# Cross-attention, two layers: row maxima sent in three parts, stack loads reordered on SyncE, bulk loads in ScalarE's queue

## The chip, the cores and the metric

One NeuronCore of a Trainium2 chip runs the whole kernel as one launch. The metric is the device time of that launch in microseconds (us). The engines are TensorE (PE in the profile; PEld is its weight load), VectorE (DVE), ScalarE (ACT), GpSimd (POOL) and SyncE (SP, which only issues DMAs). Two of them issue DMAs here, SyncE and ScalarE, each in a queue of its own over the same 16 DMA engines.

## The reference

```python
# 2 layers, batch 16, L = S = 128, D = 256, 32 query heads over 8 key/value heads, head size 8
for W in (layer0, layer1):
    q = x @ W.q + W.bq                    # (16, 128, 256)
    k = ctx @ W.k + W.bk                  # (16, 128, 64)
    v = ctx @ W.v + W.bv
    scores = einsum(q, k) / sqrt(8) + mask
    attn = softmax(scores, axis=-1)
    out = (attn @ v) @ W.o + W.bo + x
    x = layernorm(out) * gamma + beta     # the input of the next layer's q
```

The mask is all zeros for these inputs; the kernel looks at it and takes the branch without it. The context is the same in both layers.

## The kernel before, in words

A unit is one batch element of one layer: u = 0 to 31, layer 0 first. Every engine runs its own program over phases t, and the phases of the engines are tied together by semaphores alone. The order in each program is written out by hand. In phase t:

- TensorE runs the eight `scores(t, kv)`, one for each key/value head, into three banks `s_bank` (L567), four matmuls each. Between them it runs eight `scoresT` (L587), the transposed scores of the unit before, for ScalarE's exponential. At fixed places between these it runs `probs_v` of units t-3 and t-2 (L647), `transpose_max(t-1)` (L634), `project(t+3)` (L613 to L623), `project_out(t-3)` (L663) and, from phase 4 to 19, `transpose_y`.
- VectorE takes the maximum of each `s_bank` (L460). After the third of a phase it runs `max_rows(t-1)` (L468 to L471). That splits the transposed maxima of unit t-1 into three bf16 parts, high, mid and low; high has been written by ScalarE (`max_first`, L390). Each part is 32 heads by 128 columns.
- GpSimd splits q and k of unit t+3 into three bf16 parts each (L190 to L193) and does the rest of the layer norm.
- SyncE, in its iteration t, issues in this order: the rows of maxima of unit t-1 (L256), once `max_rows(t-1)` has ended; from phase 20 the result of unit t-4 (L260); the two stacks of unit t+2 (L243 and L248); the parts of unit t+3 (L228, and in layer 0 three for k, L232); and at some iterations a bulk load.

The scores are computed from stacks. q and k are each a sum of three bf16 parts, and the nine products of parts lie on 72 rows of the contraction (`TERM_ROWS`). The parts go to DRAM (`q_scratch`, `k_scratch`) and come back spread over 72 partitions: `q_stack` 576 KB, `k_stack` 144 KB for each unit, in a ring of 4 slots. `scores(u, 0)` waits for `stacks_loaded` of its slot. Rows 72 to 74 of `q_stack` hold the three parts of the maxima, with ones in `k_stack`, so that `scoresT` comes out with the maximum taken off. The first `scoresT` of unit u waits for `max_rows_loaded`; it is the last `scoresT` of phase u+1.

A DMA's wait stands on SyncE ahead of its issue, so everything behind it on SyncE waits too:

```python
need(sp, scoresT_ready, KV * (u - RING + 1))     # load_stacks(u): the slot is free
sp.wait_ge(q_stored[two], 16 * (u // 2 + 1))     # load_stacks(u): the parts are in DRAM
sp.wait_ge(maxT_step, MAXT_STEPS * (u + 1))      # load_max_rows(u): L255
sp.wait_ge(ln_step, LN_STEPS * (u + 1))          # store_y(u)
```

Of the kernel before, what the change touches and what calls it, by code (L numbers as in the profile page):

```python
# [13 lines left out]
P = 128  # L14
LAYERS, BATCH, L, S, D = 2, 16, 128, 128, 256
HEADS, KV, HD = 32, 8, 8
# [12 lines left out]
LAG = 15  # L29
AHEAD = 3  # L30
V_AHEAD = 1
X_GROUP = 4
S_BANKS = 3
INPUT_GROUPS = ((0, 1), (1, 2), (2, 4), (4, 8), (8, 12), (12, 16))
MAXT_STEPS, FLIP_STEPS, NORM_STEPS, LN_STEPS = 3, 3, 4, 4
STACK_DMAS = 2
LEAD = KT * D
VW = 4 * HD

# [9 lines left out]
def reads_before(u):  # L49

    return 6 * min(u, BATCH) + 4 * max(u - BATCH, 0)


def input_group(b):
    return next(n for n, (first, end) in enumerate(INPUT_GROUPS) if first <= b < end)


def need(engine, sem, count):
# [5 lines left out]
def cross_attention(nc, x, inputs, mask, lead, w_q1, w_kv, w_o, rows, out):  # L64
    with ExitStack() as ctx:
# [74 lines left out]
        wq1_loaded = sem("wq1_loaded")  # L140
        wkv_loaded = sem("wkv_loaded")
        bv_loaded = sem("bv_loaded")
        rows_loaded = sem("rows_loaded")
        wo_loaded = sem("wo_loaded")
        masks_loaded = sem("masks_loaded")
        x_loaded = sems("x_loaded", BATCH // X_GROUP)
        inputs_loaded = sems("inputs_loaded", len(INPUT_GROUPS))
        stacks_loaded = sems("stacks_loaded", RING)
        q_stored = sems("q_stored", 2)
        k_stored = sems("k_stored", 2)  # L150
# [59 lines left out]
        block = ctx.enter_context(nc.Block())  # L210
        rows_d = rows.rearrange("(a n) -> a n", a=LAYERS)

        def load_inputs(engine, group):
            first, end = INPUT_GROUPS[group]
            engine.dma_start(in_sb[:, first:end].rearrange("p b a k l -> p (b a k l)"),
                             inputs[:, first:end].rearrange("p b a k l -> p (b a k l)")).then_inc(inputs_loaded[group], 16)

        @block.sync
        def _(sp):
            sp.dma_start(lead_sb[:], lead).then_inc(lead_loaded, 16)  # L220
            sp.dma_start(wkv_sb[:].rearrange("p k a n -> p (k a n)"), w_kv).then_inc(wkv_loaded, 16)
            sp.dma_start(mask_sb[:].rearrange("p b s -> p (b s)"), mask).then_inc(masks_loaded, 16)
            load_inputs(sp, 2)

            def store_parts(u):
                two = u % 2
                sp.wait_ge(q_split[two], PARTS * (u // 2 + 1))
                sp.dma_start(q_scratch[u].rearrange("a p n -> p a n"), q_parts[:, two]).then_inc(q_stored[two], 16)  # L228
                if u < BATCH:
                    sp.wait_ge(k_split[two], PARTS * (u // 2 + 1))  # L230
                    for part in range(PARTS):
                        sp.dma_start(k_scratch[u, :, :, part].rearrange("a d (h s) -> (a d) h s", h=KV),  # L232
                                     k_parts[:, two, part]).then_inc(k_stored[two], 16)

            def load_stacks(u):
                layer, b = place(u)
                slot, two = u % RING, u % 2

                need(sp, scoresT_ready, KV * (u - RING + 1))
                if u < RING:  # L240
                    sp.wait_ge(k_padded, 1)
                sp.wait_ge(q_stored[two], 16 * (u // 2 + 1))
                sp.dma_start(q_stack[0:TERM_ROWS, slot].rearrange("p h l -> p (h l)"),  # L243
                             q_scratch[u].rearrange("a (d h) n -> (a d) (h n)", d=HD).unsqueeze(1)
                             .broadcast_to([PARTS * HD, PARTS, HEADS * L])).then_inc(stacks_loaded[slot], 16)
                if layer == 0:
                    sp.wait_ge(k_stored[two], 16 * PARTS * (u // 2 + 1))
                sp.dma_start(k_stack[0:TERM_ROWS, slot].rearrange("p h l -> p (h l)"),  # L248
                             k_scratch[b, layer].rearrange("d a n -> (d a) n").partition_broadcast(PARTS)
                             ).then_inc(stacks_loaded[slot], 16)  # L250

            def load_max_rows(u):
                slot, two = u % RING, u % 2
                need(sp, scoresT_ready, KV * (u - RING + 1))
                sp.wait_ge(maxT_step, MAXT_STEPS * (u + 1))  # L255
                sp.dma_start(q_stack[TERM_ROWS:STACK_ROWS, slot], max_parts[:, two]).then_inc(max_rows_loaded[two], 16)  # L256

            def store_y(u):
                sp.wait_ge(ln_step, LN_STEPS * (u + 1))
                sp.dma_start(out[u - BATCH], y[:, u % 2]).then_inc(y_left[u % 2], 16)  # L260

            for t in range(-AHEAD, UNITS + 5):
                if live(t - 1):
                    load_max_rows(t - 1)
                if BATCH <= t - 4 < UNITS:
                    store_y(t - 4)
                if live(t + 2):
                    load_stacks(t + 2)
                if live(t + AHEAD):
                    store_parts(t + AHEAD)  # L270
                if t in (-2, 2, 6):
                    load_inputs(sp, 3 + (t + 2) // 4)
                if t == 0:
                    sp.dma_start(rows_sb[:], rows_d[:, 0:3 * D].partition_broadcast(P)).then_inc(rows_loaded, 16)
                if t > 0 and t % X_GROUP == 1 and t < BATCH:
                    sp.dma_start(x_sb[:, t - 1:t - 1 + X_GROUP],
                                 x[t - 1:t - 1 + X_GROUP].rearrange("b l d -> l b d")).then_inc(x_loaded[t // X_GROUP], 16)
                if t == 1:
                    sp.dma_start(wo_sb[:].rearrange("p a k n -> p (a k n)"), w_o).then_inc(wo_loaded, 16)
                if t == 3:  # L280
                    sp.dma_start(wq1_sb[:], w_q1).then_inc(wq1_loaded, 16)

            for two in range(2):
                sp.wait_ge(y_left[two], 16 * BATCH // 2)
                sp.wait_ge(q_stored[two], 16 * UNITS // 2)
                sp.wait_ge(k_stored[two], 16 * PARTS * BATCH // 2)

        @block.gpsimd
        def _(pool):
# [39 lines left out]

            def add_bo(u):  # L330
                layer, b = place(u)
                if u == 0:
                    pool.wait_ge(rows_loaded, 16)
                if layer == 0 and b % X_GROUP == 0:
                    pool.wait_ge(x_loaded[b // X_GROUP], 16)
                if layer == 1:
                    pool.wait_ge(ln_step, LN_STEPS * (b + 1))
                need(pool, norm_step, NORM_STEPS * (u - 1) + 1)
                nc.gpsimd.tensor_tensor(x_bo[:], x_sb[:, b], rows_sb[:, layer, 0:D], ALU.add).then_inc(x_bo_ready, 1)  # L339
# [14 lines left out]
        def _(act):  # L354
# [31 lines left out]
            def max_first(u):  # L386

                act.wait_ge(maxT_ready, u + 1)
                need(act, max_rows_loaded[u % 2], 16 * (u // 2))
                nc.scalar.activation(max_parts[0:HEADS, u % 2], maxT_ps, ACT.Copy).then_inc(max_high, 1)  # L390

            def norm(u):
# [10 lines left out]
            def sum_mask():  # L403

                act.wait_ge(masks_loaded, 16)
                act.wait_ge(sum_cleared, 1)
                nc.scalar.activation(probs[:, 0, 0:KV // 2].rearrange("p h n -> p (h n)"),
                                     mask_sb[:].rearrange("p b s -> p (b s)"), ACT.Abs,
                                     accum_out=mask_sum[:, 0:1]).then_inc(sum_found, 1)

            act.wait_ge(lead_loaded, 16)
            nc.scalar.activation(bq_scaled[:], lead_sb[:, LEAD:LEAD + LAYERS * KT], ACT.Copy,
# [2 lines left out]
            for t in range(-AHEAD, UNITS + 5):  # L415
# [21 lines left out]
                exp(g + 7)  # L437
                if 0 <= t - 4 < BATCH:
                    copy_yT(t - 4)

        @block.vector
        def _(dve):
# [113 lines left out]
        def _(pe):  # L556
# [19 lines left out]
            def scoresT(g, masked):  # L576
# [5 lines left out]
                    pe.wait_ge(qk_read, reads_before(AHEAD))  # L582
                    pe.wait_ge(v_ready, 2)
                if kv == 0:
                    pe.wait_ge(max_rows_loaded[two], 16 * (u // 2 + 1))
                need(pe, exp_done, g - 1)
                mm = nc.tensor.matmul(t_bank[kv % 2][:], k_stack[0:STACK_ROWS, slot, kv],  # L587
                                      q_stack[0:STACK_ROWS, slot, GROUP * kv:GROUP * (kv + 1)],
# [7 lines left out]
            def project(u):  # L596
# [8 lines left out]
                    pe.wait_ge(qk_read, reads_before(u))  # L605
                    need(pe, v_ready, 2 * min(u - 2, BATCH))
                need(pe, yT_copied, min(u - AHEAD - 4, BATCH))
                if layer == 0 and b == INPUT_GROUPS[input_group(b)][0]:
                    pe.wait_ge(inputs_loaded[input_group(b)], 16)
                w = (lead_sb if layer == 0 else wq1_sb)[:, 0:LEAD].rearrange("p (k n) -> p k n", k=KT)  # L610
                for n in range(KT):
                    for k in range(KT):
# [40 lines left out]
            def project_out(u, t):  # L653
                layer = u // BATCH
                pe.wait_ge(flip_step, FLIP_STEPS * (u + 1))
                if u == 0:
                    pe.wait_ge(wo_loaded, 16)
                if live(t - 1):
                    pe.wait_ge(maxT_step, MAXT_STEPS * t)
                else:  # L660
                    need(pe, norm_step, NORM_STEPS * (u - 1) + 1)
                for k in range(KT):
                    mm = nc.tensor.matmul(proj_ps, attnT[:, k], wo_sb[:, layer, k], start=(k == 0), stop=(k == KT - 1))  # L663
                mm.then_inc(proj_ready, 1)
# [96 lines left out]
```

## Time and profile before

| | us |
|---|---|
| median of 3 runs | 340.6 (338.73 to 343.22) |
| the profiled execution | 340.19 |
| its span, first to last instruction | 338.3 |
| mean granted TensorE clock | 0.93 of full |

The profile is of one execution. Its span leaves out 1.9 us around the first and last instruction (340.19 - 338.3). A busy time is the sum of an engine's instructions, and what an engine waited for is put down to the event that came last. The clock is given as a share of full: 1.00 is 2.4 GHz and 0.50 is 1.2 GHz, and a value between them in a stretch is a mix of the two.

### The profile page before, as it was taken

What the parts mean: (1) busy time and instruction counts of PE and PEld (TensorE: products, weight loads), DVE (VectorE), ACT (ScalarE), POOL (GpSimd) and SP (SyncE); (2) the same over time, 40 slices, a digit from 0 to 9 for tenths busy, and PEclk for the clock granted to TensorE, in tenths of its full rate; (3) what the DMA queues carried; (4) which work ended last, traced back from release to release, by engine and by line L of the source; (5) the groups of instructions that cost most, each with busy time, mean ns of one, the idle gap of its engine ahead of it and who ended that gap; (6) DMA issues with size and microseconds to landing.
All of it is one profiled execution on the core that took longest, in us unless ns stands there. A gap on an engine that the chain in (4) does not pass through costs nothing.

```text
span 338.3 us, 8301 instructions
## 1 busy us (share of the span) xinstructions
PE 292.6 (86%) x2890; PEld 196.8 (58%) x2890; DVE 271.5 (80%) x625; ACT 209.1 (62%) x500; POOL 194.0 (57%) x335
## 2 busy tenths in 40 slices
PE   7466399599998999999899999999999999888851
PEld 4366276277666776776566666666666666554320
DVE  4426449489988998999899999999999999999441
ACT  3601257277766777777677777777777777656540
POOL 6123305366766776776656666666666666444464
PEclk9756769699999999999999999999999999999795
DMA  7584766714674446344634434444444444420000
GB/s 280 168 237 114 213 182 179 212 31 122 182 242 135 118 124 183 100 125 131 178 101 112 115 109 120 126 121 137 132 119 121 137 141 130 122 64 18 20 16 31
DMA packets 34555, 44.40 MB, mean 131 GB/s; under 512 B 11857, under 2 KB 28241, under 8 KB 31697
## 3 DMA queue, kind: packets, MB, share of 16 engines
q1 hardware_dynamic: 33952, 43.27, 44.7%
q8 instruction: 25, 0.41, 0.5%
q10 hardware_dynamic: 560, 0.59, 0.5%
q14 instruction: 18, 0.14, 0.1%
HBM read 33.10 MB, written 9.96 MB: 127 GB/s over the span
## 4 chain that ended last, share of the span: by engine, by line
PE 37%; DVE 35%; DMA 14%; issue 9%; SPq 2%; ACT 1%; POOL 1%; POOLq 0%; ACTq 0%; DVEq 0%
DVE row_max L460 18%; DMA q_stack<-max_parts 9%; PE misc_bank L663 8%; PE s_bank L567 7%; PE t_bank L587 7%; PE oT_bank L647 7%; DVE o_sb L481 4%; DMA q_scratch<-q_parts 4%; PE qkv_bank L613 3%; DVE z L499 3%; DVE attnT L492 3%; DVE max_parts L468 2%; DVE recip L487 2%; PE qkv_bank L619 2%; PE qkv_bank L623 1%
## 5 line engine op out<-in xcount | busy, mean ns | idle before, releaser
L460 DVE TENSOR_REDUCE row_max<-s_bank 128x4 f32<-128x512 f32 x256 | 168.8, 678 | 35.9 <-PE s_bank L567 35.0
L365 ACT ACTIVATE probs<-t_bank 128x512 f32<-128x512 f32 x256 | 148.0, 601 | 77.8 <-PE t_bank L587 77.4
L587 PE MATMUL t_bank<-q_stack,k_stack 75*128 75x512 bf16 x256 | 99.8, 393 | 20.4 <-DMA q_stack<-max_parts 12.6
L567 PE MATMUL s_bank<-k_stack,q_stack 72*128 72x128 bf16 x1024 | 102.3, 225 | 8.2 <-DMA k_stack<-k_scratch 7.4
L567 PEld LDWEIGHTS s_bank<-k_stack,q_stack 72*128 72x128 bf16 x1024 | 76.2, 101 | 53.1 <-issue 18.5
L307 POOL TENSOR_TENSOR rstd<-var_eps,minus_half 128x1 f32<-128x1 f32 x32 | 17.6, 548 | 56.0 <-DVE var_eps L507 56.0
L316 POOL TENSOR_TENSOR attn<-o_sb,recip 128x256 f32<-128x256 f32 x32 | 20.0, 625 | 40.0 <-DVE recip L487 39.7
L587 PEld LDWEIGHTS t_bank<-q_stack,k_stack 75*128 75x128 bf16 x256 | 25.0, 99 | 28.4 <-ACT probs L365 13.1
L663 PE MATMUL misc_bank<-wo_sb,attnT 128*128 128x256 f32 x128 | 36.0, 405 | 5.7 <-DVE attnT L492 5.7
L190 POOL TENSOR_TENSOR q_rest<-qT,q_parts 128x256 f32<-128x256 f32 x30 | 20.1, 669 | 34.4 <-ACT q_parts L374 34.4
L374 ACT ACTIVATE qT<-qkv_bank,bq_scaled 128x128 f32<-128x128 f32 x60 | 22.1, 369 | 22.6 <-PE qkv_bank L623 20.8
L647 PE MATMUL oT_bank<-probs,v_later 128*32 128x256 f32 x512 | 35.1, 393 | 0.1
L647 PE MATMUL oT_bank<-probs,v_ones 128*32 128x256 f32 x512 | 35.1, 393 | 0.0
L663 PEld LDWEIGHTS misc_bank<-wo_sb,attnT 128*128 128x128 f32 x128 | 23.5, 196 | 14.6 <-DVE attnT L492 11.9
L395 ACT ACTIVATE normed<-z,shift,rstd 128x256 f32<-128x256 f32 x32 | 19.1, 597 | 14.9 <-POOL shift L309 14.9
L323 POOL TENSOR_TENSOR scaled<-normed,rows_sb 128x256 f32<-128x256 f32 x32 | 23.3, 728 | 0.7 <-ACT normed L395 0.7
L339 POOL TENSOR_TENSOR x_bo<-x_sb,rows_sb 128x256 f32<-128x256 f32 x32 | 23.4, 732 | 0.0
L481 DVE STREAM_TRANSPOSE o_sb<-oT_bank 128x512 f32<-128x512 f32 x32 | 22.6, 707 | 0.2 <-PE oT_bank L647 0.2
L374 ACT ACTIVATE q_parts<-qkv_bank,bq_scaled 128x128 bf16<-128x128 f32 x60 | 22.4, 373 | 0.0
L647 PEld LDWEIGHTS oT_bank<-probs,v_ones 128*32 128x32 f32 x512 | 13.5, 110 | 14.5 <-issue 8.6
L647 PEld LDWEIGHTS oT_bank<-probs,v_later 128*32 128x32 f32 x512 | 13.5, 110 | 14.4 <-issue 8.2
L193 POOL TENSOR_TENSOR q_parts<-q_rest,q_parts 128x256 bf16<-128x256 f32 x30 | 20.1, 669 | 2.4
(76 smaller groups left out, 359.2 us busy)
## 6 DMA issues: line engine op xcount, KB each, us to landing
q_stack<-q_scratch SPq DMA_DIRECT2D x32, 576.0 KB
q_scratch<-q_parts SPq DMA_DIRECT2D x32, 192.0 KB, 6.2
k_stack<-k_scratch SPq DMA_DIRECT2D x32, 144.0 KB
in_sb<-inputs SPq DMA_DIRECT2D x3, 1024.0 KB, 7.9
x_sb<-x SPq DMA_DIRECT2D x4, 512.0 KB, 5.5
result<-y SPq DMA_DIRECT2D x16, 128.0 KB, 1.7
k_scratch<-k_parts SPq DMA_DIRECT2D x48, 32.0 KB, 3.5
mask_sb<-mask SPq DMA_DIRECT2D x1, 1024.0 KB, 7.2
```

The source lines that it names most:

```text
L190: engine.tensor_tensor(rest, f, parts[0], ALU.subtract).then_inc(step, 1)
L193: engine.tensor_tensor(parts[2], rest, parts[1], ALU.subtract).then_inc(step, 1)
L323: nc.gpsimd.tensor_tensor(scaled[:], normed[:], rows_sb[:, layer, D:2 * D], ALU.mult).then_inc(ln_step, 1)
L339: nc.gpsimd.tensor_tensor(x_bo[:], x_sb[:, b], rows_sb[:, layer, 0:D], ALU.add).then_inc(x_bo_ready, 1)
L365: nc.scalar.activation(probs[:, u % 2, kv], t_bank[kv % 2][:], ACT.Exp).then_inc(exp_done, 1)
L374: nc.scalar.activation(q, project_bank(u)[:, k * L:(k + 1) * L], ACT.Identity, bias=bq_scaled[:, layer * KT + k:layer * KT + k + 1], scale ...
L460: nc.vector.tensor_reduce(row_max[:, u % 2, GROUP * kv:GROUP * (kv + 1)], s_bank[(KV * u + kv) % S_BANKS][:].rearrange("p (g s) -> p g s", ...
L481: nc.vector.transpose(blocks(o_sb[:]), oT_bank[:].rearrange("p (n b l) -> p b n l", n=4, b=4)).then_inc(flip_step, 1)
L567: mm = nc.tensor.matmul(to[:, g * S:(g + 1) * S], q_stack[0:TERM_ROWS, slot, GROUP * kv + g], k_stack[0:TERM_ROWS, slot, kv], start=(g == ...
L587: mm = nc.tensor.matmul(t_bank[kv % 2][:], k_stack[0:STACK_ROWS, slot, kv], q_stack[0:STACK_ROWS, slot, GROUP * kv:GROUP * (kv + 1)], star ...
L647: mm = nc.tensor.matmul(oT_bank[32 * j:32 * (j + 1), half * 2 * L:(half + 1) * 2 * L].rearrange("p (a l) -> p a l", a=2), v, probs[:, u % ...
L663: mm = nc.tensor.matmul(proj_ps, attnT[:, k], wo_sb[:, layer, k], start=(k == 0), stop=(k == KT - 1))
```

## The change

The rows of maxima of a unit go out as three DMAs, one for each part. Each waits for its own part alone (high for ScalarE's `max_high`, mid and low for VectorE's steps) and writes one partition of `q_stack`. The k stack is loaded by three DMAs of 24 rows in place of one of 72 whose source is broadcast three times. SyncE's iteration t issues the rows of maxima of t-1, then the stacks of unit t+1 (before: t+2), then the result of unit t-4, then the parts of unit t+2 (before: t+3). The start is written out: parts and stacks of units 0 to 2 and the parts of unit 3, as before. The bulk loads behind the first (inputs from element 3 on, x, the rows of bo, gamma and beta, w_o, w_q1) move to ScalarE's queue, in smaller pieces, at the end of ScalarE's iterations. Waits on their semaphores are adapted, and waits on `max_rows_loaded` count three DMAs. TensorE, VectorE and GpSimd keep their order.

```diff
@@ constants
-X_GROUP = 4
+X_GROUP = 2
-INPUT_GROUPS = ((0, 1), (1, 2), (2, 4), (4, 8), (8, 12), (12, 16))
-STACK_DMAS = 2
+STACK_DMAS = 1 + PARTS
@@ def load_inputs
-        def load_inputs(engine, group):
-            first, end = INPUT_GROUPS[group]
-            engine.dma_start(in_sb[:, first:end].rearrange("p b a k l -> p (b a k l)"),
-                             inputs[:, first:end].rearrange("p b a k l -> p (b a k l)")).then_inc(inputs_loaded[group], 16)
+        def load_inputs(engine, b):
+            engine.dma_start(in_sb[:, b].rearrange("p a k l -> p (a k l)"),
+                             inputs[:, b].rearrange("p a k l -> p (a k l)")).then_inc(inputs_loaded[b], 16)
@@ SyncE, load_stacks and load_max_rows
-                sp.dma_start(k_stack[0:TERM_ROWS, slot].rearrange("p h l -> p (h l)"),
-                             k_scratch[b, layer].rearrange("d a n -> (d a) n").partition_broadcast(PARTS)
-                             ).then_inc(stacks_loaded[slot], 16)
+                for of_q in range(PARTS):
+                    sp.dma_start(k_stack[of_q * PARTS * HD:(of_q + 1) * PARTS * HD, slot].rearrange("p h l -> p (h l)"),
+                                 k_scratch[b, layer].rearrange("d a n -> (d a) n")).then_inc(stacks_loaded[slot], 16)
...
-                sp.wait_ge(maxT_step, MAXT_STEPS * (u + 1))
-                sp.dma_start(q_stack[TERM_ROWS:STACK_ROWS, slot], max_parts[:, two]).then_inc(max_rows_loaded[two], 16)
+                for n in range(PARTS):
+                    if n == 0:
+                        sp.wait_ge(max_high, u + 1)
+                    else:
+                        sp.wait_ge(maxT_step, MAXT_STEPS * u + (1 if n == 1 else MAXT_STEPS))
+                    sp.dma_start(q_stack[TERM_ROWS + n:TERM_ROWS + n + 1, slot],
+                                 max_parts[HEADS * n:HEADS * (n + 1), two]).then_inc(max_rows_loaded[two], 16)
@@ SyncE, the loop
-            for t in range(-AHEAD, UNITS + 5):
+            store_parts(0)
+            load_stacks(0)
+            store_parts(1)
+            load_stacks(1)
+            store_parts(2)
+            load_stacks(2)
+            store_parts(3)
+            for t in range(1, UNITS + 5):
                 if live(t - 1):
                     load_max_rows(t - 1)
+                if 3 <= t + 1 < UNITS:
+                    load_stacks(t + 1)
                 if BATCH <= t - 4 < UNITS:
                     store_y(t - 4)
-                if live(t + 2):
-                    load_stacks(t + 2)
-                if live(t + AHEAD):
-                    store_parts(t + AHEAD)
-                if t in (-2, 2, 6):
-                    load_inputs(sp, 3 + (t + 2) // 4)
-                if t == 0:
-                    sp.dma_start(rows_sb[:], rows_d[:, 0:3 * D].partition_broadcast(P)).then_inc(rows_loaded, 16)
-                if t > 0 and t % X_GROUP == 1 and t < BATCH:
-                    sp.dma_start(x_sb[:, t - 1:t - 1 + X_GROUP],
-                                 x[t - 1:t - 1 + X_GROUP].rearrange("b l d -> l b d")).then_inc(x_loaded[t // X_GROUP], 16)
-                if t == 1:
-                    sp.dma_start(wo_sb[:].rearrange("p a k n -> p (a k n)"), w_o).then_inc(wo_loaded, 16)
-                if t == 3:
-                    sp.dma_start(wq1_sb[:], w_q1).then_inc(wq1_loaded, 16)
+                if 4 <= t + 2 < UNITS:
+                    store_parts(t + 2)
@@ ScalarE, called at the end of each iteration of its loop with t > -3
+            def load_later(t):
+                if t + 5 < BATCH:
+                    load_inputs(act, t + 5)
+                if t in (0, 8):
+                    layer = t // 8
+                    act.dma_start(rows_sb[:, layer],
+                                  rows_d[layer:layer + 1, 0:3 * D].partition_broadcast(P)).then_inc(rows_loaded[layer], 16)
+                if 0 < t < BATCH and t % X_GROUP == 1:
+                    act.dma_start(x_sb[:, t - 1:t - 1 + X_GROUP],
+                                  x[t - 1:t - 1 + X_GROUP].rearrange("b l d -> l b d")).then_inc(x_loaded[t // X_GROUP], 16)
+                if t in (2, 10):
+                    layer = t // 10
+                    act.dma_start(wo_sb[:, layer].rearrange("p k n -> p (k n)"),
+                                  w_o[:, layer * LEAD:(layer + 1) * LEAD]).then_inc(wo_loaded[layer], 16)
+                if t == 9:
+                    act.dma_start(wq1_sb[:], w_q1).then_inc(wq1_loaded, 16)
```

## Rows read from the trace of the kernel before

**Rows 1.** The page's section 2, the span in 40 slices: TensorE busy, its clock.
```profile
PE   7466399599998999999899999999999999888851
...
PEclk9756769699999999999999999999999999999795
```
**Rows 2.** The waits of the whole span: us in total, times, longest.
```profile
DVE row_max L460 <- PE s_bank L567: 35.0, 49, 4.4
...
PE t_bank L587 <- DMA q_stack<-max_parts: 12.6, 6, 5.0
...
PE s_bank L567 <- DMA k_stack<-k_scratch: 7.4, 2, 5.3
```
**Rows 3.** The waits of SyncE's queue, whole span.
```profile
SPq L255 <- DVE max_parts L471: 96.9, 28, 6.7
...
SPq L242 <- DMA q_scratch<-q_parts: 20.6, 17, 4.0
```
**Rows 4.** Timeline of phases 29 and 30: start, duration, engine, line.
```profile
290.44 0.28 DVE L471 TENSOR_TENSOR max_parts<-misc_bank,max_parts 32x128 bf16<-32x128 f32 x1
...
290.80 0.76 SPq L256 DMA_DIRECT2D q_stack<-max_parts  x1
...
292.64 0.80 SPq L243 DMA_DIRECT2D q_stack<-q_scratch  x1
...
293.49 0.71 SPq L248 DMA_DIRECT2D k_stack<-k_scratch  x1
...
293.99 0.39 PE L567 MATMUL s_bank<-k_stack,q_stack 72*128 72x128 bf16 x4
...
299.28 0.74 SPq L256 DMA_DIRECT2D q_stack<-max_parts  x1
```
**Rows 5.** Stretches behind those loads: length, busy times, PEclk, DMA share, GB/s.
```profile
294.15:297.15 3.00, 3.00 (x39) 1.76 (x37) 2.93 (x8) 1.83 (x4) 0.65 (x2) 1.00 0.74 197
297.15:299.65 2.50, 1.46 (x22) 0.63 (x20) 2.40 (x7) 2.16 (x4) 1.35 (x3) 1.00 0.19 66
```
**Rows 6.** SyncE's issues by line: ns least/median/most.
```profile
L243 SPq DMA_DIRECT2D q_stack<-q_scratch x32: 801/832/927, 11.9 to 292.6; - x32
L248 SPq DMA_DIRECT2D k_stack<-k_scratch x32: 708/720/747, 13.1 to 293.5; - x32
L260 SPq DMA_DIRECT2D result<-y x16: 332/354/361, 215.8 to 336.0; - x16
```
**Rows 7.** Stretches with a gap on TensorE, columns as in rows 5.
```profile
93.00:94.00 1.00, 0.24 (x2) 0.23 (x3) 0.97 (x3) 0.00 (x0) 1.00 (x3) 1.00 0.62 164
...
63.00:64.00 1.00, 0.00 (x0) 0.00 (x0) 0.00 (x0) 0.00 (x0) 0.00 (x0) 0.50 0.72 208
...
313.00:314.00 1.00, 0.39 (x1) 0.10 (x1) 0.94 (x3) 0.58 (x3) 0.78 (x3) 1.00 0.00 0
314.00:315.00 1.00, 0.01 (x1) 0.01 (x1) 0.93 (x4) 1.00 (x3) 1.00 (x2) 1.00 0.00 0
315.00:316.00 1.00, 1.00 (x9) 0.37 (x13) 0.17 (x1) 0.83 (x2) 0.86 (x2) 0.54 0.00 0
```
**Rows 8.** Timeline of phase 4: its first scores, and the maxima issued in it.
```profile
64.46 0.63 PE L567 MATMUL s_bank<-k_stack,q_stack 72*128 72x128 bf16 x4
...
70.97 0.78 SPq L256 DMA_DIRECT2D q_stack<-max_parts  x1
```
**Rows 9.** Timeline of SyncE and TensorE: the first phases, and phase 31.
```profile
33.69 0.77 SPq L274 DMA_DIRECT2D rows_sb<-rows  x1
34.49 0.79 SPq L256 DMA_DIRECT2D q_stack<-max_parts  x1
...
41.49 0.59 PE L587 MATMUL t_bank<-q_stack,k_stack 75*128 75x512 bf16 x1 [5.04 <-DMA q_stack<-max_parts]
...
57.02 0.78 SPq L256 DMA_DIRECT2D q_stack<-max_parts  x1
...
307.76 0.75 SPq L256 DMA_DIRECT2D q_stack<-max_parts  x1
```

More of the change, by code:

```diff
@@ L51, in reads_before @@
     return 6 * min(u, BATCH) + 4 * max(u - BATCH, 0)
-def input_group(b):
-    return next(n for n, (first, end) in enumerate(INPUT_GROUPS) if first <= b < end)
 def need(engine, sem, count):
@@ L142, in cross_attention @@
         bv_loaded = sem("bv_loaded")
-        rows_loaded = sem("rows_loaded")
-        wo_loaded = sem("wo_loaded")
+        rows_loaded = sems("rows_loaded", LAYERS)
+        wo_loaded = sems("wo_loaded", LAYERS)
         masks_loaded = sem("masks_loaded")
         x_loaded = sems("x_loaded", BATCH // X_GROUP)
-        inputs_loaded = sems("inputs_loaded", len(INPUT_GROUPS))
+        inputs_loaded = sems("inputs_loaded", BATCH)
         stacks_loaded = sems("stacks_loaded", RING)
@@ L331, in add_bo @@
                 layer, b = place(u)
-                if u == 0:
-                    pool.wait_ge(rows_loaded, 16)
+                if b == 0:
+                    pool.wait_ge(rows_loaded[layer], 16)
                 if layer == 0 and b % X_GROUP == 0:
@@ L388, in max_first @@
                 act.wait_ge(maxT_ready, u + 1)
-                need(act, max_rows_loaded[u % 2], 16 * (u // 2))
+                need(act, max_rows_loaded[u % 2], 16 * PARTS * (u // 2))
                 nc.scalar.activation(max_parts[0:HEADS, u % 2], maxT_ps, ACT.Copy).then_inc(max_high, 1)
@@ L439, in _ @@
                     copy_yT(t - 4)
+                if -AHEAD < t:
+                    load_later(t)
         @block.vector
@@ L584, in scoresT @@
                 if kv == 0:
-                    pe.wait_ge(max_rows_loaded[two], 16 * (u // 2 + 1))
+                    pe.wait_ge(max_rows_loaded[two], 16 * PARTS * (u // 2 + 1))
                 need(pe, exp_done, g - 1)
@@ L607, in project @@
                 need(pe, yT_copied, min(u - AHEAD - 4, BATCH))
-                if layer == 0 and b == INPUT_GROUPS[input_group(b)][0]:
-                    pe.wait_ge(inputs_loaded[input_group(b)], 16)
+                if layer == 0:
+                    pe.wait_ge(inputs_loaded[b], 16)
                 w = (lead_sb if layer == 0 else wq1_sb)[:, 0:LEAD].rearrange("p (k n) -> p k n", k=KT)
@@ L655, in project_out @@
                 pe.wait_ge(flip_step, FLIP_STEPS * (u + 1))
-                if u == 0:
-                    pe.wait_ge(wo_loaded, 16)
+                if u % BATCH == 0:
+                    pe.wait_ge(wo_loaded[layer], 16)
                 if live(t - 1):
```

## The prediction

> **What bounds the kernel now.** I read the page's slices first, then the waits, then one phase of the timeline. The slices show two stretches [rows 1]: up to about 66 us TensorE is often idle and its clock is down, and from there on it is busy nine tenths at full clock. The waits put the early loss down to transfers [rows 2]: the first `scoresT` of a unit waits for the rows of maxima (12.6 us, one wait of 5.0), the scores wait for the k stack (7.4 us, one of 5.3), and VectorE's 35.0 us of waiting for scores lie behind these. After that no stack is late. A phase takes 8.48 us (299.28 - 290.80, from one issue of the maxima to the next) [rows 4]. TensorE and VectorE share that bound.
>
> Call M the time at which SyncE can issue the last part of the maxima in phase t, and A the time at which `scores(t+1, 0)` starts. The timeline gives both [rows 4]: VectorE's last step of the split starts at 290.44, M is 290.80, A is 293.99 and the next M 299.28. So M to A is 3.2 us and A to M is 5.3 us. SyncE's longest wait is this M: 96.9 us over 28 phases [rows 3]. It is harmless as long as nothing urgent is queued behind it.
>
> **The reordering.** This is the part that decides. Before, the stacks issued behind M of phase 29 are those of unit 31: q at 292.64, k at 293.49 [rows 4]. They are needed at `scores(31, 0)`, one phase after 293.99, that is at 293.99 + 8.48 = 302.47. That leaves 9.8 us from the q issue. The changed kernel issues in the same place, behind all three waits on the maxima, the stacks of unit 30. They are needed at 293.99, 3.2 us after M. The loads can't be on time, because their chain is now a loop: M, the two stacks, `scores(t+1, 0)`, the first three maxima of phase t+1, `max_rows(t)`, next M. Its length becomes the phase. I sum it.
>
> 1. *The issue of the last part.* Not in the trace with 32 partitions on one side and one on the other. The nearest rows are the issues of 0.35 us (result) and 0.76 us (all three parts, 290.80) [rows 4, 6]. The part before may still be issuing, up to 0.2 us. 0.35 to 0.95, taken 0.6.
> 2. *From the q issue to both stacks landed.* The q data is on the engines from 294.15 to about 297.15, 1.5 us after its issue started. The stretch moved 3.00 x 197 = 590 KB. A tail follows until 299.65 at 66 GB/s and a share of 0.19, which is 3 of 16 engines: the k load [rows 5]. So today k lands 7.0 us after the q issue (299.65 - 292.64). The change cuts k in three loads of 24 rows. If they spread as the q load does, 720 KB at the 197 GB/s of that stretch is 3.7 us, and at half as much again 2.4 us, so 1.5 + 2.4 to 1.5 + 3.7. The three k issues end 0.83 + 3 x (0.35 to 0.72) = 1.9 to 3.0 us after the q issue began [rows 6], and need about 1 us more to land, which lies inside. 3.9 to 5.2, taken 4.7. Without the spreading it is 7.0.
> 3. *A to M.* 5.3 us [rows 4], with VectorE still working off the phase before. Starved VectorE starts at once, which can save 0.3. 5.0 to 5.3, taken 5.1.
>
> The phase at full clock is 0.6 + 4.7 + 5.1 = 10.4 us. From M of phase 3 (57.02) to M of phase 31 (307.76) lie 28 phases of 8.96 us on average [rows 9]. They cost 28 x (10.4 - 8.96) = +40 us.
>
> That the three-engine tail goes is the change's gain, and a page explains it. The Trainium skill (DMA: Bandwidth & Descriptors, the section on why a DMA increments its semaphore by 16) says a DMA runs on the largest number of engines up to 16 that divides the outermost sizes of both sides: 3 for the broadcast k load and for the rows of maxima, 12 for 24 rows, 16 for a part of 32 heads. The share of 0.19 in the tail agrees with it.
>
> **The clock.** Between the end of TensorE's work of a phase, at about A as it is now, and the late A there is a new gap of 0.6 + 4.7 - 3.2 = 2.1 us in every phase. What a gap does, three places show [rows 7]. One of about 1.1 us (0.24 busy in 93 to 94, begun shortly before 93) left the clock at 1.00. One of about 1.6 us (0.39 and 0.01 busy in 313 to 315) was followed by 0.54. One of 3.5 us was at 0.50 before work came back. At the low level A to M took 6.5 us (64.46 to 70.97) [rows 8] against 5.1, so a phase that starts cold costs 1.4 more: 11.8 us. I take a phase in two cold, 0.7 us, since a gap of 2.1 lies above the one that lost the clock, but not by much. Phase 11.1 us, 28 x (11.1 - 8.96) = +60 us. Bounds: none cold +40, all cold 28 x (11.8 - 8.96) = +80.
>
> The Trainium skill (TensorE: Matmul & The Clock Gate, HAM oscillation) describes a kernel in which each wait for a transfer drops the clock anew, in every tile. By that all phases would be cold. The gap of 1.6 us above, with its fall, speaks for it; that of 1.1 us is too short to speak against it.
>
> **The start.** Parts and stacks of units 0 to 2 keep their order. Removed ahead of the first M are the inputs of four elements (1 MB) and the three rows (issue 0.77 us, 768 KB), which are directly ahead of the first maxima: issued at 34.49, waited for until 41.49, 7.0 us [rows 9]. In late phases such rows are needed just ahead of A, about 3 us after M [rows 4], and come in time. So up to 4 us there, as much again for the earlier stack loads, and the low clock they cause. I take -8 us at M of phase 3, bounds -3 and -14. The bytes still pass the same 16 engines, only from another queue, so it can be little.
>
> **What costs nothing.** Maxima issued part by part: high and mid leave up to 1 us earlier, but the low part leaves at M as before, and the wait is for all three. Where the rows came late behind a bulk load (part of the 12.6 us [rows 2]) it no longer matters under the loop. ScalarE issues 26 bulk DMAs at 0.35 to 0.83 us, as those of [rows 6], some 15 us over layer 0, while it waits for TensorE anyway, the more so in longer phases; if it were not hidden, one exponential would be late by one issue, about 0.5 us in 13 phases. The result store is now behind the stacks, so its wait no longer holds them; the parts are stored one iteration later, but their load also is, and the gap between the two is again a whole phase (waits of 20.6 us there before [rows 3], mostly at the start). Smaller bulk loads keep up: input b is issued two phases ahead of `project(b)`. w_o of layer 0 is issued at the end of phase 2 and used late in phase 3; it may be late once by 1 us. The end, from M of phase 31, stays.
>
> **Sum.** Against the profiled execution: 340.2 - 8 + 60 = 392 us. It stands 0.4 under the median of 340.6, which changes nothing.
>
> **Rivals.**
> - *All phases cold.* 340.2 - 8 + 80 = 412 us. For it the 1.6 us gap; against it the 1.1 us one. Chance 0.15.
> - *The k loads don't spread, so the change doesn't do what its 24 rows say.* Then step 2 is 7.0, the phase 0.6 + 7.0 + 5.1 = 12.7 at full clock and 14.1 cold: 340.2 - 8 + 28 x 3.7 = 436, or 475 cold. For it: nothing shows a 24-row load. Against it: q, also over 24 outer rows at its source, moved 197 GB/s. Chance 0.10.
> - *The loop is short enough, and the kernel is not slower.* The point is M to A of 3.2 to 3.6 us, against my 5.3. Then every phase is 8.48 us, 28 phases take 237.4 in place of 250.7, and the start gains too: 340.2 - 13 - 8 = 319 us. Halfway, with all terms at their low end (0.35 + 3.9 + 5.0 = 9.25, +8 us), it is 340 us. Against it: 576 KB alone kept the engines busy for most of 3 us behind 1.5 us of start. Chance 0.07, of which 0.03 faster by over 2%, 0.03 within 2% and the rest slower.
> - The forecast, between none cold and three phases in four cold: 0.68.
>
> **Range.** Lower end: none cold with the loads near their quick end, 340.2 - 10 + 28 x 1.1 = 361. Upper end: all cold and a start that gains only 3, with the slow bound of step 2 in part, 340.2 - 3 + 88 = 425. It leaves out most of the last two rivals, under 2 in 10. Slower by over 2% (about what a measurement of this kernel tells from no change) 0.94, within 0.03, faster 0.03.
>
> **What would show it.** In the new profile SyncE's q-stack issue should stand 0.5 to 1 us behind the last of the three maxima, with the k issues behind it. The waits should have a large new entry in every phase, scores on the DMA of `k_stack` or `q_stack`, some 2 us each, 50 us or more in all, and VectorE's wait on scores should grow likewise. The chain should run through SyncE and the stack DMA in each phase. The tail at a share of 0.19 should be gone. The clock should dip in late phases, and maxima issues should be 10.5 to 12 us apart. The first issue of a low part should come some us ahead of 34.49. I am wrong if the stacks of unit t+1 leave SyncE before M of phase t, or land within 3 us of it.

## The result

The changed kernel takes 469.1 us (median of 4 runs, 465.6 to 472.0) against 339.7 us before: ratio 1.388, 95% interval 1.380 to 1.397. It is slower, as forecast, but by 129 us where 52 were predicted; 469 lies outside the range of 361 to 425. The profiled execution took 465.6 us and has a span of 463.8 us. Some executions of a kernel run slower than its others at a lower granted clock; medians here are over all runs and ratios over the fast ones alone, so a ratio is not quite the quotient of two medians.

The slices of the page after the change, the same rows as [rows 1]:

```profile
PE   6578788678769777787788666678776668777881
...
PEclk9577979889897988877777889987877988666786
```

The loss is not at the start but in every phase: TensorE is mostly busy six to eight tenths up to the end, and its clock dips all along. The waits (engine, line, what it waited for: us in total, times, longest) show on what, against [rows 2]:

```profile
DVE row_max L475 <- PE s_bank L582: 155.1, 120, 4.4
...
PE s_bank L582 <- DMA k_stack<-k_scratch: 101.1, 30, 5.3
```

30 waits for a stack, nearly one for each unit, of 3.4 us on average. And the wait of `scoresT` for the maxima, 12.6 us before, is down to one of 1.6 us. The page's chain now has `DMA k_stack<-k_scratch` at 31% and SyncE's queue at 14% of the span. One phase of the timeline shows the loop, against [rows 4]:

```profile
300.84 0.40 PE L582 MATMUL s_bank<-k_stack,q_stack 72*128 72x128 bf16 x4 [3.78 <-DMA k_stack<-k_scratch]
...
304.67 2.38 SPq L254 DMA_DIRECT2D q_stack<-max_parts  x3
...
306.13 0.28 DVE L486 TENSOR_TENSOR max_parts<-misc_bank,max_parts 32x128 bf16<-32x128 f32 x1
...
307.15 0.84 SPq L237 DMA_DIRECT2D q_stack<-q_scratch  x1
...
314.31 0.61 PE L582 MATMUL s_bank<-k_stack,q_stack 72*128 72x128 bf16 x4 [4.06 <-DMA k_stack<-k_scratch]
```

Read it in three pieces. From the first scores (300.84) to the low part (306.41) 5.6 us; from there to the q issue (307.15) 0.7; from the q issue to the next first scores (314.31) 7.2. The next phase begins where this one ends, so the phase is 13.5 us. From the low part of phase 3 to that of phase 31 the 28 phases take 380.2 us, 13.58 each, against 8.96 before, and the pieces are 5.97, 0.80 and 6.81 us on average.

### The profile page after: what moved, and what is told of

Same layout as the page of the kernel before. It is cut to its first block, busy times and chain, and to the rows that moved or that the text cites. A ratio compares the mean times of both kernels' runs of the same rounds, so it can differ in the third digit from the quotient of the medians.

```text
span 463.8 us, 8455 instructions
## 1 busy us (share of the span) xinstructions
PE 343.1 (74%) x2890; PEld 222.1 (48%) x2890; DVE 277.7 (60%) x625; ACT 211.8 (46%) x500; POOL 194.2 (42%) x335
## 4 chain that ended last, share of the span: by engine, by line
PE 35%; DMA 33%; SPq 14%; DVE 10%; issue 5%; POOL 1%; ACT 1%; POOLq 0%; ACTq 0%; DVEq 0%
DMA k_stack<-k_scratch 31%; PE oT_bank L662 12%; PE s_bank L582 9%; PE t_bank L602 7%; SPq L243 6%; SPq L237 4%; PE qkv_bank L628 4%; DVE o_sb L496 3%; SPq L254 2%; DVE row_max L475 2%; DMA k_scratch<-k_parts 1%; SPq L226 1%; DVE max_parts L486 1%; DVE max_parts L483 1%; DVE recip L502 1%
## 5 line engine op out<-in xcount | busy, mean ns | idle before, releaser
L360 ACT ACTIVATE probs<-t_bank 128x512 f32<-128x512 f32 x256 | 149.5, 600 | 196.5 <-PE t_bank L602 196.4
L582 PE MATMUL s_bank<-k_stack,q_stack 72*128 72x128 bf16 x1024 | 117.9, 249 | 102.3 <-DMA k_stack<-k_scratch 101.1
L582 PEld LDWEIGHTS s_bank<-k_stack,q_stack 72*128 72x128 bf16 x1024 | 84.7, 112 | 170.2 <-DMA k_stack<-k_scratch 109.5
L602 PE MATMUL t_bank<-q_stack,k_stack 75*128 75x512 bf16 x256 | 115.5, 455 | 4.4 <-ACT probs L360 2.7
L662 PE MATMUL oT_bank<-probs,v_later 128*32 128x256 f32 x512 | 47.1, 500 | 0.1
L662 PE MATMUL oT_bank<-probs,v_ones 128*32 128x256 f32 x512 | 42.4, 458 | 0.0
L602 PEld LDWEIGHTS t_bank<-q_stack,k_stack 75*128 75x128 bf16 x256 | 28.8, 114 | 8.5 <-ACT probs L360 6.0
L662 PEld LDWEIGHTS oT_bank<-probs,v_later 128*32 128x32 f32 x512 | 15.8, 129 | 20.6 <-issue 15.4
L628 PEld LDWEIGHTS qkv_bank<-in_sb,wq_sb 128*128 128x128 f32 x128 | 23.3, 253 | 1.2
L662 PEld LDWEIGHTS oT_bank<-probs,v_ones 128*32 128x32 f32 x512 | 14.9, 121 | 18.0 <-issue 14.0
```

Of the source, the lines that this page charges most:

```text
L360: nc.scalar.activation(probs[:, u % 2, kv], t_bank[kv % 2][:], ACT.Exp).then_inc(exp_done, 1)
L582: mm = nc.tensor.matmul(to[:, g * S:(g + 1) * S], q_stack[0:TERM_ROWS, slot, GROUP * kv + g], k_stack[0:TERM_ROWS, slot, kv], start=(g == ...
L628: mm = nc.tensor.matmul(to[:, n * L:(n + 1) * L], w[:, k, n * P:(n + 1) * P], in_sb[:, b, 0, k], start=(n == 0 and k == 0), stop=(k == KT ...
L662: mm = nc.tensor.matmul(oT_bank[32 * j:32 * (j + 1), half * 2 * L:(half + 1) * 2 * L].rearrange("p (a l) -> p a l", a=2), v, probs[:, u % ...
```

## The experiments

The kernel before was run again beside the others: 340.3 us beside experiments 1 to 4, 340.8 beside 5 to 8, 341.1 beside 9 to 12. Ratios are to it, with the 95% interval. The pieces of a phase are means over the same 28 phases each time.

**1. The old order alone.**

```diff
-                if 3 <= t + 1 < UNITS:
-                    load_stacks(t + 1)
                 if BATCH <= t - 4 < UNITS:
                     store_y(t - 4)
-                if 4 <= t + 2 < UNITS:
-                    store_parts(t + 2)
+                if live(t + 2):
+                    load_stacks(t + 2)
+                if live(t + AHEAD):
+                    store_parts(t + AHEAD)
```

> The changed kernel with SyncE's old order alone: in iteration t the maxima of t-1, the result of t-4, the stacks of t+2, the parts of t+3. Three DMAs of maxima, three k loads and the bulk in ScalarE's queue stay. If the loop through the late stacks is the whole loss (low part, q issue, stacks landed, first three maxima, low part: 13.6 us a phase in 28 phases against 8.96), the phases fall back to 8.5 to 8.8 us and the time to 322 to 336 us, a little under the kernel before, because the start keeps its gain of about 5 us. If the many small DMAs (26 on ScalarE, 96 of maxima, 96 of k) cost something of their own, it stays above 345 us.

Measured 327.4 us, ratio 0.967 (0.958 to 0.976); phases of 8.73 us. So the whole loss, 142 us, hangs on SyncE's order, and the other parts of the change together are a gain.

**2. The new order alone**, the same edit the other way round in the kernel before.

> The kernel before with the new order of SyncE alone: maxima of t-1 in one DMA, stacks of t+1 with k in one broadcast load, result, parts of t+2; bulk in SyncE's queue. Loop theory: the same loop, with the k load on 3 engines at its end. From the q issue to the stacks landed 7.0 to 8 us in place of 6.6, phase about 14.2 us, 340 + 28 x 5.2 = 486 us. If instead the three-part DMAs are what delays the landing, this one comes out clearly under the changed kernel, 400 to 450 us.

Measured 507.3 us, ratio 1.509 (1.494 to 1.525). The order alone costs 167 us, 21 more than forecast. The stretches behind one pair of loads (length, busy times, clock, DMA share, GB/s; q issued at 400.16, first scores at 407.69):

```profile
403.00:406.00 3.00, 0.56 (x6) 0.22 (x4) 1.45 (x3) 0.60 (x1) 0.37 (x1) 1.00 0.73 199
406.00:407.50 1.50, 0.00 (x0) 0.00 (x0) 0.00 (x0) 0.00 (x0) 0.00 (x0) 0.50 0.19 73
```

The tail of the k load at a share of 0.19, hidden before [rows 5], is now waited for with every engine idle. From the q issue to the first scores it is 7.61 us on average, the phase 14.72.

**3. Tiny stores.**

```diff
-                sp.dma_start(q_scratch[u]..., q_parts[:, two]).then_inc(q_stored[two], 16)
+                if u < RING:
+                    sp.dma_start(q_scratch[u]..., q_parts[:, two]).then_inc(q_stored[two], 16)
+                else:
+                    sp.dma_start(q_scratch[u, 0, :, 0:8], q_parts[:, two, 0, 0:8]).then_inc(q_stored[two], 16)
...
-                             q_scratch[u]...
+                             q_scratch[u % RING]...
...
-                sp.dma_start(out[u - BATCH], y[:, u % 2])...
+                sp.dma_start(out[u - BATCH, :, 0:8], y[:, u % 2, 0:8])...
```

> The changed kernel with the stores of the q parts from unit 4 on cut to 8 columns of one part, the loads reading the parts of unit u mod 4, and the result store cut to 8 of 256 columns (so most of the result is left out and the later units use the q of others). Loads keep their sizes and places. If the 320 KB of stores issued right behind the stacks share the engines with them and make them late, the 6.6 us from q issue to the first scores shrink by 1.3 us or more, the phase to 12.2 us or less, the time to about 430 us. If the landing is set by the loads themselves (start 2.1 to 2.4 us after the issue, then 720 KB), nothing much changes: 455 to 470 us.

Measured 462.1 us, ratio 1.373 (1.364 to 1.381). The theory of the stores fell: up to 320 KB less behind the loads are worth 7 us in all. From the q issue to the first scores it is still 6.65 us. With the stores out of the way one load can be followed by its bytes (q issued at 358.32, first scores at 364.95):

```profile
358.32:359.75 1.43, 1.43 (x26) 0.81 (x19) 1.27 (x3) 1.11 (x5) 1.43 (x3) 1.00 0.07 14
359.75:364.25 4.50, 1.68 (x13) 1.11 (x10) 2.49 (x5) 1.65 (x3) 1.90 (x3) 0.90 0.69 165
364.25:364.95 0.70, 0.00 (x1) 0.01 (x1) 0.00 (x0) 0.00 (x0) 0.00 (x0) 0.50 0.00 0
```

1.4 us until the first bytes, 4.5 us for 4.5 x 165 = 743 KB, and 0.7 us in which nothing moves and the scores have not begun.

**4. TensorE kept busy ahead of the wait.**

```diff
+                need(pe, max_done, n - S_BANKS + 1)
                 if kv == 0:
+                    if u >= AHEAD:
+                        for _ in range(14):
+                            nc.tensor.matmul(to[:], awake[:, 0:P], awake[:], start=True, stop=True, skip_group_check=True)
                     pe.wait_ge(stacks_loaded[slot], 16 * STACK_DMAS * (u // RING + 1))
-                need(pe, max_done, n - S_BANKS + 1)
```

> The changed kernel with 14 matmuls of 512 columns (about 3 us) on zeros ahead of the wait for the stacks, from unit 3 on, so that the gap on TensorE is filled. They write the bank that the scores then overwrite. If the low clock after the gap makes the way from first scores to low part 6.2 us in place of 5.4, the phase falls by about 0.8 us and the time by about 22 us, to 445 us, with a granted clock of 0.95 or more. If the low clock is hidden behind the loop, the time stays at 465 to 472 us.

Measured 442.8 us, ratio 1.311 (1.294 to 1.327): 26 us less than the changed kernel, with more work. One phase of its timeline:

```profile
310.77 2.97 PE L582 MATMUL s_bank<-awake 128*128 128x512 bf16 x13
...
314.69 0.40 PE L585 MATMUL s_bank<-k_stack,q_stack 72*128 72x128 bf16 x4 [0.95 <-DMA k_stack<-k_scratch]
```

The clock is held: its mean over the span is 0.944 against 0.814, and four of the scores' matmuls take 0.40 us here where they took 0.61 at 314.31 in the changed kernel. From the first scores to the low part it is 5.03 us in place of 5.97 (4.96 in nearly every phase), the phase 12.75 in place of 13.58. From the q issue to the first scores next to nothing changes (6.77 against 6.81).

**5. One k load in the new kernel.**

```diff
-                for of_q in range(PARTS):
-                    sp.dma_start(k_stack[of_q * PARTS * HD:(of_q + 1) * PARTS * HD, slot]...,
-                                 k_scratch[b, layer].rearrange("d a n -> (d a) n")).then_inc(stacks_loaded[slot], 16)
+                sp.dma_start(k_stack[0:TERM_ROWS, slot].rearrange("p h l -> p (h l)"),
+                             k_scratch[b, layer].rearrange("d a n -> (d a) n").partition_broadcast(PARTS)
+                             ).then_inc(stacks_loaded[slot], 16)
```

> The changed kernel with k in one broadcast load again (3 engines by the share of 0.19). Loop theory: the k tail is now in the loop. From the q issue to the first scores 7.6 us, as in the run with the new order alone, in place of 6.8; phase 14.4 us; 469 + 28 x 0.8 = 491 us. If the 24-row loads are no faster (the rival that they don't spread), it stays at 469 us.

Measured 507.0 us, ratio 1.493 (1.479 to 1.506), 38 us over the changed kernel and 16 over the expectation. The landing is nearly as expected: 7.72 us from the q issue to the first scores, where 7.6 was expected. The phase is 14.68, since the other two pieces grew too (6.10 and 0.86), and the low part of phase 3 is done at 59.1 us against 52.1. So the 24-row loads do what they say, and are worth 1.1 us a phase inside the loop, 31 us over 28 phases; the other 7 us are lost by the low part of phase 3.

**6. Stacks ahead of the maxima, the unit unchanged.**

```diff
-                if live(t - 1):
-                    load_max_rows(t - 1)
                 if 3 <= t + 1 < UNITS:
                     load_stacks(t + 1)
+                if live(t - 1):
+                    load_max_rows(t - 1)
```

> The changed kernel, where iteration t issues the stacks of t+1 ahead of the waits on the maxima of t-1, still one unit later than before. The wait on this phase's maxima leaves the loop, but the parts of t+1 are stored only in iteration t-1, so the loop runs over two phases: low part, about 3.2 us of issues, 4.7 us of store, 6.8 us of load, 5.9 us to the low part after next, 20.6 us for two phases or 10.3 each. Time about 340 - 5 + 28 x 1.4 = 375 us. If the order within an iteration were all that mattered, it would be 327 us as with the old order; if the distance in units alone, 465 us.

Measured 336.1 us, ratio 0.991 (0.982 to 0.999). Two statements swapped give back 133 of the 142 us. I had expected 375. The timeline of one phase shows what was wrong in that:

```profile
244.00 1.06 SPq L222 DMA_DIRECT2D q_scratch<-q_parts  x1
...
246.82 0.84 SPq L237 DMA_DIRECT2D q_stack<-q_scratch  x1
...
249.26 2.60 SPq L254 DMA_DIRECT2D q_stack<-max_parts  x3
...
250.93 0.28 DVE L486 TENSOR_TENSOR max_parts<-misc_bank,max_parts 32x128 bf16<-32x128 f32 x1
...
254.63 0.39 PE L582 MATMUL s_bank<-k_stack,q_stack 72*128 72x128 bf16 x4
```

The q stack leaves at 246.82, which is 4.4 us before the low part is done (251.21), and the scores of its unit run at 254.63, 7.8 us later, without a wait. The store ahead of it was done in 2.8 us (244.00 to 246.82). I had used the 4.7 us that stores take in the changed kernel, where they lie behind the stack loads in the queue; ahead of them they take a median of 2.4. The wait that makes the loop is the one on this phase's maxima, not the distance in units; the 9 us that are still missing to experiment 1 are the most that the distance can cost.

**7. Half the q stack** (from unit 4 on; the first four units keep the whole load).

```diff
+                    sp.dma_start(q_stack[0:TERM_ROWS, slot, 0:HEADS // 2].rearrange("p h l -> p (h l)"),
+                                 q_scratch[u]...[:, 0:HEADS * L // 2].unsqueeze(1)
+                                 .broadcast_to([PARTS * HD, PARTS, HEADS * L // 2])).then_inc(stacks_loaded[slot], 16)
```

> The changed kernel with half of the q stack (16 of 32 heads, 288 KB) loaded from unit 4 on, the other half left as it was in its slot, so the scores of those heads are not those of their unit. If the 6.8 us from q issue to first scores are mostly bytes at some 170 GB/s, they fall by 1.7 us, the phase to 11.9 us, the time to about 421 us. If they are mostly fixed time (start and completion), the time stays above 455 us.

Measured 397.5 us, ratio 1.168 (1.157 to 1.179), 24 under the expectation. The phase is 11.12 us, 2.46 less. Behind a q issue at 253.63:

```profile
253.63:255.00 1.37, 1.37 (x21) 0.54 (x19) 1.34 (x3) 1.37 (x5) 1.37 (x3) 1.00 0.11 20
255.00:257.50 2.50, 2.25 (x19) 1.56 (x17) 1.80 (x4) 1.52 (x4) 1.87 (x3) 1.00 0.69 225
```

The start of 1.4 us stays and the bytes take less: the first scores come at 258.09, 4.5 us after the issue. On average it is 4.93 us, so 1.9 us went with the bytes, where 1.7 was expected. The rest is the first piece, 5.30 in place of 5.97: the wait was shorter (0.84 us before these scores) and the clock stood higher (mean 0.906 against 0.814).

**8. The kernel before with three DMAs of maxima and three k loads**, in the old order with the bulk on SyncE.

> The kernel before with the three DMAs of maxima and the three k loads alone: old order, bulk in SyncE's queue in large pieces. Against the run with the old order and everything else changed (327 us) it tells the bulk loads' part. If the gain of 13 us comes from the k loads and maxima, 326 to 330 us; if from the bulk that stood ahead of maxima and stacks, 337 to 340 us. I expect 333, some of each.

Measured 336.0 us, ratio 0.988 (0.976 to 0.999). That is 5 us under the kernel before, with an interval that all but reaches no change.

The last four are all in the old order with the bulk on ScalarE.

**9. The kernel of experiment 1 again.**

> The same kernel as the first run with the old order, again, beside the next three: 327 us, 0.96 to 0.97 of the kernel before.

Measured 328.1 us, ratio 0.966 (0.960 to 0.972).

**10. The maxima in one DMA** (edit: one wait for `MAXT_STEPS * (u + 1)`, one DMA of 3 rows, as before).

> Old order, bulk on ScalarE, three k loads, but the maxima in one DMA of 96 rows once all are ready. If the parts' early issue and their spread over 16 engines is worth something, it shows where scoresT waits for the maxima in the first 150 us: 3 to 6 us, so 330 to 333 us. If it is worth nothing, 327 us or one less, since SyncE issues 0.8 us a phase instead of 2.4.

Measured 327.6 us, ratio 0.962 (0.956 to 0.968). The same as 9 within the intervals: the three-part issue is worth nothing that can be measured here, and costs nothing.

**11. One k load** (the edit of 5 in this order).

> Old order, bulk on ScalarE, maxima in three, but k in one broadcast load with its tail on 3 engines. With a phase of slack the tail (2.5 us) is hidden once the phases run: 327 to 329 us. In the first phases each stack is waited for and lands about 0.8 us later, three times, and the store behind it lands later: up to 333 us.

Measured 339.1 us, ratio 0.996 (0.992 to 1.000). A miss: without the 24-row loads 11 of the 13 us of gain are gone, though the stacks have a phase of slack. Once the phases run, what TensorE waits for is not a stack: its waits for one are all in the first 30 us (7.8 us in two, against 5.3 in one). It is the maxima. First this run, then experiment 9:

```profile
PE t_bank L595 <- DMA q_stack<-max_parts: 11.7, 11, 3.7
```

```profile
PE t_bank L595 <- DMA q_stack<-max_parts: 4.1, 5, 1.9
```

The loss lies in layer 0. The low part of phase 4 is done at 66.4 us against 60.4, which is half of it; up to phase 15 a phase takes 9.81 us against 9.05, and from there on 8.50 against 8.55, with the same k load still in every phase. The maxima do not leave late: SyncE still waits for their high part 24 times. They land later, a median of 3.0 us after their issue against 2.6. That they queue behind the k tail on the same engines fits all this. But SyncE's wait for the stored q parts grew as well, to 41.9 us from 22.5, and neither was tried by itself: the cause of these 11 us stays open.

**12. The result store behind stacks and parts.**

> Old distance in units with everything else changed, and the result store moved behind stacks and parts in the iteration, so that its wait (28.7 us in 16 phases) holds nothing. The phases of layer 1 are at 8.48 us already, set by TensorE and VectorE, so nothing is gained: 326 to 328 us. If that wait had a cost, up to 4 us less.

Measured 330.4 us, ratio 0.970 (0.964 to 0.977). No gain, as expected.

## Why the prediction was right in kind and wrong in size

**The reordering: right.** Experiments 1, 2 and 6 show it from three sides. The new order alone costs 167 us in the kernel before, the old order takes 142 us off the changed one, and 133 of these come back when the stacks only pass the waits on the maxima. The chain of pieces is as the prediction wrote it down.

**Step 2, the issue of q to both stacks landed: the step that failed.** It was taken as 4.7 us with a slow bound of 5.2 and measured 6.81. Over 28 phases the 2.1 us are 59 us, most of the 74 missing between 392 and the profiled 465.6. Two things were left out, which experiment 3 shows on one load. First, the term ended with the last byte; the scores began 0.7 us after it. Second, 720 KB were moved at a peak rate: my 4.7 left 3.2 us for them, 225 GB/s, and they take 4.5 us at 165. The 197 GB/s of [rows 5] came from a stretch that ended at the k tail, so it had the fast part of a load and not its end. The rows had a warning: before the change, k landed 7.0 us after the q issue, and I let 24-row loads take 2.3 us off that. Experiment 5 gives what they really take off, 0.9 us (7.72 - 6.81).

**The clock: near in size, off in its picture.** The prediction had 5.1 us at full clock and 0.7 for one phase in two begun cold at 1.4 each, 5.8 in all; measured are 5.97. The price was right: phases that begin at 0.50 take 6.46 us, against 4.96 with the clock held. But TensorE waited 3.4 us on average and not 2.1, since step 2 was longer, and the clock fell in 25 of the 28 phases: in 12 before the first scores, in 13 behind them. One of each kind, from its first scores on, with the clock ahead of the last two columns:

```profile
301.00:302.00 1.00, 1.00 (x17) 0.54 (x19) 0.72 (x2) 0.51 (x1) 0.00 (x0) 0.96 0.00 0
302.00:303.00 1.00, 1.00 (x15) 0.22 (x4) 0.21 (x2) 0.09 (x1) 0.58 (x2) 0.50 0.00 0
...
314.00:315.00 1.00, 0.69 (x5) 0.45 (x5) 0.04 (x1) 0.00 (x0) 0.00 (x0) 0.50 0.09 26
```

The phase of 314.31 began at 0.50, that is 1.2 GHz. That of 300.84 began at full clock behind a wait of 3.78 us, and lost it a microsecond later with TensorE busy. The length of a wait alone does not tell which it will be: the scores at 190.84 began at 1.00 behind 2.87 us, those at 203.06 at 0.50 behind 2.12 us. Experiment 4 prices the whole: 26 us, against 20 predicted. The Trainium skill (TensorE: Matmul & The Clock Gate, HAM oscillation) describes a kernel in which the wait for a transfer drops the clock anew in every round; this trace agrees in 25 phases of 28, though in 13 of them only behind the first scores.

**Step 1, the start, the end.** Low part to q issue 0.80 us against 0.6, +6 us over 28 phases. SyncE starts the last part's issue within 0.1 us of the low part (306.47 behind 306.41), that issue takes 0.59, and the q issue begins 0.1 later. The start gained less: the low part of phase 3 is done at 52.1 against 57.0, 5 us against 8. The end, from the low part of phase 31, is 31.5 us against 30.6. So the miss of 74 us is 59 of step 2, 6 of step 1, 5 of the clock, 3 of the start and 1 of the end. The terms as measured give 338.3 - 4.9 + 28 x (13.58 - 8.96) + 0.9 = 464 us, the span.

**What costs nothing.** Right for the result store (experiment 12), for the maxima in three (10), and for ScalarE's 26 issues, with which experiment 1 is 13 us under the kernel before. The rival "the k loads don't spread" fell with experiment 5, though its time, 436 to 475 us, holds the measured one: the right time for a wrong reason. The rival "not slower" needed the first scores 3.2 to 3.6 us after the maxima could be issued; they came 7.6 us after (0.80 + 6.81).

**The edits apart.** In the old order the 24-row k loads with maxima in three are worth 5 us with the bulk on SyncE (experiment 8), and the bulk on ScalarE with maxima in three 2 us without the 24-row loads (experiment 11; its interval touches no change). All together give 13, more than the 5 and the 2; why is not shown. The best version run is the changed kernel in the old order, 328 us, 0.966 of the kernel before, with the maxima in three DMAs or in one (experiments 9 and 10).

## What to carry to other kernels

In a queue that issues in order, ask of each wait what stands behind it and when that is needed: a load behind a wait on this phase's results can't be early, however long its data has been ready. Here two statements in the other order are worth 133 us of 469. When a load moves from hidden to waited for, size it to the first instruction that uses it, with the start, the end of its slowest part and the time after the last byte, not with the rate of its busiest stretch. And a loop through a transfer brings gaps on TensorE, so add the price of its clock at once.

## What the runs showed of the hardware that was not expected

- How long a DMA takes to issue does not go by its bytes. In the changed kernel (ns least/median/most of one issue):

```profile
L254 SPq DMA_DIRECT2D q_stack<-max_parts x96: 502/536/672, 32.1 to 440.6; - x96
L243 SPq DMA_DIRECT2D k_stack<-k_scratch x96: 311/365/532, 14.0 to 420.9; - x96
```

  So 8 KB of maxima take 0.54 us, where all 24 KB took 0.76 before [rows 4], and a k load of 24 rows 0.37 us, where the one of 72 took 0.72 [rows 6]: three take longer than one, 1.6 and 1.1 us. The store of 128 KB of results takes 0.35 [rows 6]. The 2.38 us for three at 304.67 hold waits between them.
- A load that is hidden by a whole phase of slack can still cost: with k in one load (tail on a share of 0.19) the kernel was 11 us slower, all of it in layer 0, and the maxima were waited for 11 times and 11.7 us in place of 5 times and 4.1 us (experiments 11 and 9).
- The same store of q parts (192 KB) lands a median of 2.4 us after its issue when it is ahead of the stack loads (experiment 6) and 4.7 us when it is behind them (the changed kernel).
- TensorE's clock can fall while TensorE is busy, a microsecond behind a wait (302 us in the changed kernel, as above).
